# Full-width context tiles on PE and one DVE reduction for the cross attention's row sums

## The reference, cut

```python
q  = ln(fp8_linear(ln_out, wq));   k = ln(fp8_linear(ln_out, wk));   v = fp8_linear(ln_out, wv)
core = softmax(q @ k.T / sqrt(128)) @ v              # 256 queries x 256 keys
qx = ln(fp8_linear(ln_out, wqx))
kx, vx = split(cond @ w_kv_x.T);  kx = ln(kx)        # cond: 64 context rows
xout = softmax(qx @ kx.T / sqrt(128)) @ vx           # 256 queries x 64 keys
x = x + tanh(g) * fp8_linear(concat(core, xout), wproj)
# then: layernorm, top-2 of 8 experts and a shared expert, gated, added to x
```

## Time and profile before

| | us |
|---|---|
| median of 3 runs | 961.87 (960.19 to 961.93) |
| the profiled execution | 961.15 |
| its span on the core | 959.3 |
| busy PE / DVE / ACT / POOL | 832.0 / 785.0 / 753.3 / 734.5 |
| instructions of PE / DVE / ACT / POOL | 6406 / 1792 / 2433 / 570 |

### The profile page before, as it was taken

How to read it: one execution, slowest core, us unless ns; L and a number is a source line. 1 busy time by engine, 2 the same in 40 slices (tenths; PEclk the granted TensorE clock), 3 DMA queues, 4 the chain that set the end, 5 groups by cost and what they waited for, 6 DMA issues and landing times.

```text
span 959.3 us, 21100 instructions
## 1 busy us (share of the span) xinstructions
PE 832.0 (87%) x6406; PEld 625.0 (65%) x6406; DVE 785.0 (82%) x1792; ACT 753.3 (79%) x2433; POOL 734.5 (77%) x570
## 2 busy tenths in 40 slices
PE   0377799999999999999999999999998747788795
PEld 0255467777777777777777777778776325566553
DVE  7899888888888888888888889888887886854356
ACT  3377699999999999999999999999997641343331
POOL 4498799889979988997998999899897236444653
PEclk9697799999999999999999999999999779999998
DMA  9421434224323422522342252234228623678963
GB/s 251 126 88 45 100 58 81 56 56 98 61 55 62 97 55 55 102 57 55 67 92 55 55 104 55 55 72 87 55 55 198 174 75 75 147 170 168 191 173 103
DMA packets 226348, 90.64 MB, mean 94 GB/s; under 512 B 202592, under 2 KB 219968, under 8 KB 226304
## 3 DMA queue, kind: packets, MB, share of 16 engines
q1 hardware_dynamic: 218448, 77.78, 36.9%
q0 software_dynamic: 7856, 12.33, 6.3%
HBM read 31.88 MB, written 10.22 MB: 44 GB/s over the span
## 4 chain that ended last, share of the span: by engine, by line
PE 65%; DVE 15%; ACT 7%; issue 5%; DMA 5%; POOL 2%; SPq 1%; DVEq 0%; ACTq 0%; POOLq 0%
PE S L513 11%; PE A L418 8%; PE A L419 8%; PE T L484 6%; PE S L501 5%; PE JB L543 5%; DMA psrc<-w_lo 4%; PE VB L410 3%; PE VB L412 2%; PE VB L411 2%; PE T L534 2%; DVE stage L1128 2%; ACT zq L781 2%; PE T L411 1%; PE T L412 1%
## 5 line engine op out<-in xcount | busy, mean ns | idle before, releaser
L1637 POOL TENSOR_TENSOR rstd<-var,mhalf 128x8 f32<-128x8 f32 (+1 forms) x128 | 191.1, 1508 | 67.2 <-DVE var L1206 66.8
L418 PE MATMUL A<-w_hi,xq 128*128 128x256 f16 (+1 forms) x1024 | 188.1, 250 | 35.6 <-DVE v_lo L1180 21.1
L419 PE MATMUL A<-w_lo,xq 128*128 128x256 f16 (+1 forms) x1024 | 188.0, 250 | 0.0
L1192 DVE TENSOR_SCALAR qT<-T,qmap 128x512 f32<-128x512 f32 x128 | 103.4, 808 | 62.0 <-PE T L484 62.0
L513 PE MATMUL S<-kT,qT 128*128 128x256 f32 x512 | 141.0, 399 | 5.7 <-ACT probx L907 3.4
L1164 DVE TENSOR_REDUCE nmx<-S 128x2 f32<-128x512 f32 (+1 forms) x192 | 114.6, 597 | 23.2 <-PE S L513 23.0
L418 PEld LDWEIGHTS A<-w_hi,xq 128*128 128x128 f16 x1024 | 101.5, 99 | 46.8 <-issue 30.2
L899 ACT ACTIVATE prob<-S,nmx 128x256 f32<-128x256 f32 x256 | 119.6, 485 | 11.2 <-DVE nmx L1164 10.0
L1704 POOL TENSOR_TENSOR raw<-raw,rstd 128x1024 f32<-128x1024 f32 x64 | 126.4, 1975 | 0.0
L1688 POOL TENSOR_TENSOR prob<-prob,rl 128x1024 f32<-128x1024 f32 x64 | 121.0, 1891 | 0.0
L513 PEld LDWEIGHTS S<-kT,qT 128*128 128x128 f32 x512 | 89.5, 193 | 40.1 <-issue 14.1
(11 more groups left out here) (251 smaller groups left out, 2392.1 us busy)
## 6 DMA issues: line engine op xcount, KB each, us to landing
stage<-wallT SPq DMA_DIRECT2D x8, 1024.0 KB, 5.0
yd<-pT SPq DMA_DIRECT2D x46, 128.0 KB
wp<-wpT POOLq DMA_DIRECT2D x1, 2048.0 KB, 30.9
zd<-zr SPq DMA_DIRECT2D x8, 256.0 KB, 2.4
out<-xs SPq DMA_DIRECT2D x8, 256.0 KB, 2.2
xs<-x SPq DMA_DIRECT2D x1, 1792.0 KB, 21.2
raw<-w13T SPq DMA_DIRECT2D x2, 704.0 KB, 4.7
sq<-w13T SPq DMA_DIRECT2D x2, 704.0 KB, 4.4
```

What stands on the lines that cost most here:

```text
L418: nc.tensor.matmul(o, l, w_hi[:, c, col:col + n], start=(c == 0), stop=False)
L419: last = nc.tensor.matmul(o, l, w_lo[:, c, col:col + n], start=False, stop=(c == HC - 1))
L1192: nc.vector.tensor_scalar(qT[:, p, k, :, :].rearrange("p h s -> p (h s)"), o[:, :], qmap[:, 2 * k:2 * k + 1], qmap[:, 2 * k + 1:2 * k + 2] ...
L1637: return nc.gpsimd.tensor_tensor(dst, src, mhalf[:, 0:n], ALU.pow)
```

## The change

Three things in PE's tiles: the 64 context keys are transposed as a full 128 x 128 tile (the zero rows with them; only the first 64 columns are read), the low part of the context's V keeps its lower 64 rows at zero (a memset at the start; `low_vx` writes rows 0 to 63 only), and the second matmul of `pv_cross` takes all 128 rows. In `exp_cross` the four activations leave out the accumulator. DVE gets `sums_x`, one reduction of the four cross blocks of 64 for each of the 128 rows, ahead of `sums`, which then waits for it, on DVE's own semaphore.

```diff
--- before.py
+++ after.py
@@ -490,7 +490,7 @@
                     done(pe, d_qT, n)
                     for t in range(ST):
                         nc.tensor.transpose(T1[:, t * P:(t + 1) * P], raw[:, p, UK + t, :], idt[:, :])
-                    nc.tensor.transpose(T1[:, S:KT], raw[0:SC, p, UKX, :], idt[0:SC, 0:SC]).then_inc(mm_kT, 1)
+                    nc.tensor.transpose(T1[:, S:S + P], raw[:, p, UKX, :], idt[:, :]).then_inc(mm_kT, 1)
 
                 def scores_cross(n, p):
                     done(pe, d_qxT, n)
@@ -531,7 +531,7 @@
                         done(pe, a_xo, n - 1)
                     both = pT[:, p, PX0:PX0 + PJ, :].rearrange("p j s -> p (j s)")
                     nc.tensor.matmul(T1[:, :], vx_hi[:, vg, :], both, start=True, stop=False)
-                    nc.tensor.matmul(T1[:, :], vx_lo[0:SC, vg, :], both[0:SC], start=False, stop=True).then_inc(mm_xo, 1)
+                    nc.tensor.matmul(T1[:, :], vx_lo[:, vg, :], both, start=False, stop=True).then_inc(mm_xo, 1)
 
                 def project_out(n, p, og):
                     done(pe, d_cq, n)
@@ -905,7 +905,7 @@
                     done(act, d_plx, n - 2)
                     for j in range(PJ):
                         last = nc.scalar.activation(probx[:, p, j, :], S0[:, j * SC:(j + 1) * SC], ACT.Exp,
-                                                    bias=nmx[:, p, 4 + j:5 + j], accum_out=lsum[:, p, 4 + j:5 + j])
+                                                    bias=nmx[:, p, 4 + j:5 + j])
                     last.then_inc(a_ex, 1)
 
                 def turned(n, p, lag):
@@ -1182,7 +1182,7 @@
 
                 def low_vx(n):
                     done(dve, a_vxh, n)
-                    nc.vector.scalar_tensor_tensor(vx_lo[:, g, :], T0[:, D:2 * D], VSCALE / WSCALE, vx_hi[:, g, :], ALU.mult,
+                    nc.vector.scalar_tensor_tensor(vx_lo[0:SC, g, :], T0[0:SC, D:2 * D], VSCALE / WSCALE, vx_hi[0:SC, g, :], ALU.mult,
                                                    ALU.subtract).then_inc(d_vx, 1)
 
                 def read_q(n, p, k):
@@ -1211,8 +1211,13 @@
                 def variances_k(n, p):
                     variances(n, p, slice(UK, NU), d_ss, g_rstd, d_var)
 
+                def sums_x(n, p):
+                    done(dve, a_ex, n)
+                    nc.vector.tensor_reduce(lsum[:, p, 4:8], probx[:, p, :, :], AX.X, ALU.add).then_inc(d_sumx, 1)
+
                 def sums(n, p):
-                    done(dve, a_ex, n)
+                    done(dve, d_sumx, n)
+                    done(dve, a_e1, n)
                     done(dve, g_norm, n - 2)
                     nc.vector.reciprocal(rl[:, p, :], lsum[:, p, :]).then_inc(d_rl, 1)
 
@@ -1243,11 +1248,13 @@
                         low_p(n0 - 3, par(3))
                         low_px(n0 - 3, par(3))
                         for k in range(2): maxima(n0 - 1, par(1), k)
+                        sums_x(n0 - 2, par(2))
                         sums(n0 - 2, par(2))
                         read_logits(0, 0, NE, A1)
                         done(dve, mm_kT, STEPS - 1)
                         best(0, 0, NE, 0)
                         maxima(n0 - 1, par(1), 2)
+                        sums_x(n0 - 1, par(1))
                         sums(n0 - 1, par(1))
                         low_p(n0 - 2, par(2))
                         low_px(n0 - 2, par(2))
@@ -1296,6 +1303,7 @@
                 if live(n0 - 1): maxima(n0 - 1, par(1), 0)
                 if live(n0): low_v(n0)
                 if live(n0 - 1): maxima(n0 - 1, par(1), 1)
+                if live(n0 - 2): sums_x(n0 - 2, par(2))
                 if live(n0 - 2): sums(n0 - 2, par(2))
                 if between:
                     if isinstance(n0, int) and n0 == 0:
@@ -1319,6 +1327,7 @@
             dve.wait_ge(ld_x0, 16)
             front1(0)
             nc.vector.memset(raw[:, :, UKX, :], 0.0)
+            nc.vector.memset(vx_lo[SC:P, :, :], 0.0)
             nc.vector.memset(sq[:, :, UKX, :], 0.0)
             nc.vector.memset(xs[:, B * ST:, :], 0.0)
             for e in range(E):
```

More of the change, by code:

```diff
@@ L243, in build @@
             sem("a_" + n) for n in "q0 sq1 q1 sqk v vxh x kT e0 e1 ex ph phx core xo".split())
-        d_v, d_vx, d_ssq, d_ss, d_varq, d_var, d_qT, d_qxT, d_m0, d_m1, d_mx, d_rl, d_pl, d_plx, d_clip, d_cq, d_x1 = (
-            sem("d_" + n) for n in "v vx ssq ss varq var qT qxT m0 m1 mx rl pl plx clip cq x1".split())
+        d_v, d_vx, d_ssq, d_ss, d_varq, d_var, d_qT, d_qxT, d_m0, d_m1, d_mx, d_rl, d_pl, d_plx, d_clip, d_cq, d_x1, d_sumx = (
+            sem("d_" + n) for n in "v vx ssq ss varq var qT qxT m0 m1 mx rl pl plx clip cq x1 sumx".split())
         g_rstdq, g_uq, g_rstd, g_u, g_normx, g_norm = (sem("g_" + n) for n in "rstdq uq rstd u normx norm".split())
```

## The result

| | us |
|---|---|
| kernel before, median of 4 runs on this chip | 961.03 (959.78 to 961.93) |
| changed kernel, median of 4 runs | 980.24 (978.21 to 987.15) |
| ratio, 95% interval | 1.0228 (1.0184 to 1.0271) |
| the profiled execution, its span | 982.27, 980.5 |

The account below looks back on a forecast made before the run. PE was taken as the bound, with ACT, POOL and DVE close behind. 0.67 us per block, 4.7 over seven, plus 0.1 in the first block, less 0.7 at start and end: 4.1 saved, 957.8 us; range 951 to 962.

Parts of the forecast that it names:

- What bounds: All eight batches flowing, 544 us: PE busy 539, ACT 532, POOL 489, DVE 475; one engine's saving limited by the next.
- PE, gross: Gaps around PE's 64-row tiles: 0.20 us at the key transposes, 0.30 at the cross matmuls, 0.50 a tick.
- What is late next: PE's wait for ACT's key map absorbs the transposes' 0.20; a plain tick keeps 0.30 and takes 9.93 us.
- POOL's pairs: T0 to T2 and T5 to T7: POOL's unedited chain sets these tick pairs, 20.58 and 20.59 us, gain 0.
- T0 to T2 shrinks: Sign of a wrong prediction: the two ticks from a block's first cross-query transposes shorten, so POOL's chain has unseen slack.
- Tick 2 to 4: PE waits for DVE's scalings; the new reduction leaves no gain up to there, then a plain tick: net 0.27 us.
- T7 to T8: Tick 7 of a block, where DVE's rounding stands beside POOL's roots: 0.10 us to gain.
- Start: First block: reductions cost 0 to 2.5 us, vx_lo memset 0 to 1.7, PE gains up to 1.3; taken as +0.5.
- the paragraph on ACT and DVE: ACT's four dropped accumulator reads, 0.37 us a tick, gain nothing; DVE's reduction costs 0.42, with room in plain ticks.
- Rival 3: T5 to T7: the new reduction makes DVE's `ve` miss POOL's gap, 1.4 us longer; kernel 967.4, chance 0.10.
- Rivals 1 and 4: 1: kT chain gives way, plain tick 9.8, 955.6, chance 0.14. 4: PE's gaps stay, 965, chance 0.04.

Follow-up runs that it names:

- experiment 2: The changed kernel with 80 waits on an already arrived semaphore put on ACT ahead of its loop, no work changed; 951.95 us (kernel before 958.88), ratio 0.9948.
- experiments 7 and 8: Against the kernel before: 7, full-width transposes of the cross keys alone, 985.10 us, ratio 0.9985; 8, full-width low half of the cross context alone, 980.13 us, ratio 0.9942.
- experiment 1: Against the kernel before: only the PE part of the change, with ACT's accumulator reads kept and no sums_x; 953.44 us (before 958.88), ratio 0.9944.
- experiment 3: The kernel before with 40 waits on ACT ahead of its loop, none of the change in it; 986.86 us (before 958.88), ratio 1.0306.
- 6: The changed kernel with ACT's accumulator reads kept in the first block alone, no filler; 981.29 us where the kernel before takes 986.45, ratio 0.9939.
- experiment 9: The changed kernel with 140 waits on ACT ahead of its loop; 977.29 us (kernel before 958.55), ratio 1.0178.
- experiment 5: The changed kernel with 40 waits on ACT ahead of its loop; 1029.95 us on a chip where the kernel before takes 986.45, ratio 1.0442.

## Why the prediction was wrong

**Where the 29.6 us are.** From T8 to T64 the changed kernel takes 608.7 us, the kernel of experiment 2 579.1, the kernel before 586.6. So the change as costed gives 7.4 back, and the displaced loop takes 29.6. Of these:

- The first ticks are 22.6 longer in all. The wait on ACT is 4.1 - 0.8 = 3.3 us each time; where PE keeps its clock, the tick is 2.9 longer for it (12.84 and 12.82, for 9.97 in experiment 2), so 0.4 is slack. Six times 2.9 is 17.2.
- In four of the six first ticks PE also loses clock, and these are another 1.3 to 1.5 longer (14.15 to 14.30), 5.4 in all. Windows of the changed kernel around the first one (columns as above, the clock third from the end):

```profile
232.00:234.50 2.50, 0.70 (x6) 0.68 (x7) 0.00 (x1) 1.59 (x4) 1.06 (x1) 1.00 0.57 159
234.50:237.00 2.50, 2.50 (x24) 2.38 (x22) 2.15 (x3) 1.79 (x6) 0.00 (x0) 0.56 0.00 0
237.00:239.50 2.50, 2.50 (x15) 2.08 (x16) 1.80 (x7) 2.20 (x5) 1.37 (x1) 0.75 0.01 3
```

  PE had stood idle for 2.5 us and then worked for 1.0; then the granted clock goes to the lower of its two levels, 1.2 GHz, and comes back within the window after. At that level the cross scores (line 501) start 0.213 apart, at the other 0.112. PE was idle for 2.5 us in all six first ticks, so the idle stretch alone doesn't say which of them lose clock.
- 7.0 in the two ticks behind them (T1 to T3). The stall moves DVE against POOL, and `ve` at 244.63 (shown above) comes just behind the start of POOL's line 1697. Timeline of POOL:

```profile
244.51 1.89 POOL L1697 TENSOR_TENSOR prob<-prob,rl 128x1024 f32<-128x1024 f32 x1
```

  It takes until that has ended, 1.79 us. In experiment 2, with the same reduction, it stands ahead of that line, beside the shorter one in front of it (1691 there), and takes a quarter, until that one has ended. Timelines of DVE and POOL:

```profile
240.01 0.46 DVE L1076 SCALAR_TENSOR_TENSOR ve<-mv,epst 128x2 f32<-128x2 f32 x1
```

```profile
239.85 0.61 POOL L1691 TENSOR_TENSOR probx<-probx,rl 128x256 f32<-128x256 f32 x1
```

  With no POOL instruction beside it, at the start of each kernel, `ve` takes 0.16.

**Step by step.** *What bounds*: right. *PE, gross*: right, 0.20 and 0.30; the gaps went with the 64-row tiles. *What is late next*: right, 9.93 against 9.91, and experiments 7 and 8 split it as told, 0.02 and 0.31. *POOL's pairs*: a little off, and by one of the signs that I had named, that T0 to T2 shrinks. I took 20.58 and 20.59 as fixed; they became 20.48 and 20.44, so 0.25 a block more than forecast. POOL's 15.80 us from the roots on were not all its own work: its line 1644 took 1.33 us before and takes 1.17 in experiment 2; why was not looked for. *Tick 2 to 4*: 0.36 for 0.27. *T7 to T8*: 0.10, as said. A block gains 1.02, not 0.67. *Start*: T8 came 1.65 later, at 147.09 for 145.44, not 0.5. With the low half alone it stands at 147.12, with the transposes alone at 145.72, with the reductions alone at 145.23, which points to the memset of `vx_lo` rather than to the reductions. But experiment 1 has the memset and stands at 146.12, and experiment 3, without it, at 146.21, so this stays open.

**The step that failed** is in the paragraph on ACT and DVE: "so I cost the gain at nothing". I bounded the removal of ACT's reads between nothing and a gain of 24 us, and excluded a loss without a reason. An instruction that is removed also moves all that stand behind it, here the loop of ACT, and that cost six waits of 3.3 us and what followed from them, 29.6 us in all. None of my rivals had this mechanism. Rival 3 had the right neighbour, `ve` against POOL, but with the wrong trigger and in tick 5; it came as a consequence, at the end of DVE's ticks 0 and 1, and makes a quarter of the loss. Its account of the 0.64 us of `ve` in the earlier trace rows was not quite so either: beside it runs POOL's line 1681, which ends at 376.65, and `ve` lasts until that has ended (376.67). Rivals 1 and 4 are refuted by the plain tick (9.91, neither 9.8 nor 10.23).

**What was right but hidden.** With the loop in place, the change is worth what was forecast: ratio 0.9948 and 0.9939 for a forecast of 957.8 / 961.9 = 0.9957. All of that is PE's low half (0.9942 alone). The reductions on DVE cost 0.25 a block by themselves, and with the PE part 82.63 against 82.54. The best kernels are therefore 1, 2, 6 and 8, which the runs do not tell apart; 8 is the smallest edit.

## What to carry over

When an edit adds or removes instructions in a program with a loop, count them per engine and compare the list of instruction fetches before and after; a loss that begins with the second pass, with "issue" as the releaser of the loop's first instruction, points to the loop's place and not to the work. Before such an edit is judged, its kernel is worth a run with the loop moved back by filler. And when the cost of a removal is bounded from below by nothing, ask what else was held in place by what is removed.

## What the runs showed of the hardware

- ACT fetches instructions in pieces of 8 KB, 128 instructions. A loop over three pieces ran without any fetch in its passes but the one of SP; over four it fetched five times a pass, and its first step came 3.8 to 6.6 us behind the branch for 0.8. PE's loop, 1,383 recorded instructions a pass before the change, showed none in any kernel here; its own queue has 22 fetches of 16 KB each time, all ahead of the loop's first back-edge or behind its exit.
- Moving an unchanged loop by 20 instructions, with 40 waits on a semaphore that had arrived, made the kernel 3.1% slower.
- 2.5 us of idle PE were followed by the 1.2 GHz level in four of six cases in the changed kernel, five of six in experiment 3 and two of six in experiment 9; 4.7 to 5.0 us, in experiment 5, in six of six.
- A `ve` of 128 x 2 elements on DVE took 0.16 us with no POOL instruction beside it, 0.46 beside one of 0.61 and 1.79 behind the start of one of 1.89, the last two until POOL's had ended. DVE's line 1174 (128 x 256) went from 0.41 to 2.12 in the same way.
